# Logits folded into the scores and sums products of a routed decoder layer

## What is computed

```
x = x + linear_attention(layernorm(x))            # 8 heads of 64, elu + 1 features
x = x + cross_attention(layernorm(x), ctx) @ Wout + bout
h = layernorm(x)
logits = h @ Wg.T                                 # 8 experts
top_v, top_i = top_k(logits, 2); gates = softmax(top_v)
pos = cumsum(onehot(top_i)) - 1; keep = pos < 1280
x = x + sum over the two experts of gate * expert(h)   # gelu(h W1a) * (h W1b) @ W2
```

## Time and profile before

| | us |
|---|---|
| runs: median (lowest to highest of 3) | 1612.87 (1607.64 to 1614.09) |
| the profiled execution | 1614.39 |
| its span, first to last instruction | 1612.7 |

### The profile page before, as it was taken

The page is one execution under the profiler, slowest core; times in us unless marked ns, Lnnn a source line. Parts: engine busy times, 40 slices in busy tenths (PEclk is TensorE's granted clock), DMA queues, the critical chain, the costliest instruction groups (busy, mean ns, idle before and its releaser), DMA issues.

```text
span 1612.7 us, 21589 instructions
## 1 busy us (share of the span) xinstructions
PE 1507.6 (93%) x7686; PEld 1271.4 (79%) x7687; DVE 662.7 (41%) x1393; ACT 542.6 (34%) x881; POOL 360.3 (22%) x354
## 2 busy tenths in 40 slices
PE   6999999899998549999999989999999999999998
PEld 5778877788876338788888968888978978898886
DVE  6635555576777614331143243114532332214311
ACT  5334333244433414331143243124432332124311
POOL 3213123135543520201211220121121121021011
PEclk9999999998998569999999999999999999999999
DMA  9101222044424431521233252123452162024122
GB/s 190 53 1 52 80 79 105 1 157 132 99 85 131 131 105 54 157 60 31 37 121 91 52 145 70 33 33 117 124 159 46 36 175 46 20 52 130 22 43 26
DMA packets 78987, 132.23 MB, mean 82 GB/s; under 512 B 30388, under 2 KB 30516, under 8 KB 77912
## 3 DMA queue, kind: packets, MB, share of 16 engines
q1 hardware_dynamic: 62520, 97.40, 20.6%
q0 software_dynamic: 16416, 34.16, 11.4%
HBM read 93.63 MB, written 37.91 MB: 82 GB/s over the span
## 4 chain that ended last, share of the span: by engine, by line
PE 82%; DVE 5%; issue 3%; DMA 3%; POOL 3%; ACT 2%; another core or an unknown queue 1%; SPq 0%; ACTq 0%; POOLq 0%; DVEq 0%
PE pg L877 15%; PE pg L878 15%; PE pg L879 15%; PE pj L877 9%; PE pj L879 8%; PE pj L878 8%; PE pj L1079 2%; POOL slot_table L574 2%; PE pg L1048 1%; PE pg L1128 1%; PE pt L1226 1%; DMA stage<-w 1%; DVE w_lo L1289 1%; PE pt L1070 1%
## 5 line engine op out<-in xcount | busy, mean ns | idle before, releaser
L877 PE MATMUL pg<-xe_hi,w_hi 128*128 128x512 f32 (+2 forms) x1088 | 393.9, 362 | 22.4 <-issue 10.6
L878 PE MATMUL pg<-xe_lo,w_hi 128*128 128x512 f32 (+2 forms) x1088 | 393.1, 361 | 0.0
L879 PE MATMUL pg<-xe_hi,w_lo 128*128 128x512 f32 (+2 forms) x1088 | 392.6, 361 | 0.0
L1641 DVE TENSOR_TENSOR hp<-gl,pg 128x512 f32<-128x512 f32 (+1 forms) x136 | 87.1, 641 | 606.1 <-ACT gl L830 596.1
L632 POOL DMA_INDIRECT out_rows<-ost,etab x62 | 100.3, 1618 | 800.0 <-ACT ost L857 396.3
L877 PEld LDWEIGHTS pg<-xe_hi,w_hi 128*128 128x128 f32 x1088 | 207.6, 191 | 54.2 <-issue 12.2
L879 PEld LDWEIGHTS pg<-xe_hi,w_lo 128*128 128x128 f32 x1088 | 207.7, 191 | 28.3
L830 ACT ACTIVATE gl<-pg 128x512 f32<-128x512 f32 (+1 forms) x136 | 76.1, 560 | 457.0 <-PE pg L879 452.7
L878 PEld LDWEIGHTS pg<-xe_lo,w_hi 128*128 128x128 f32 x1088 | 207.5, 191 | 28.3
L877 PE MATMUL pj<-w_hi,hg_hi 128*128 128x512 f32 x464 | 183.4, 395 | 0.0
L879 PE MATMUL pj<-w_hi,hg_lo 128*128 128x512 f32 x464 | 180.8, 390 | 0.0
(11 more groups left out here) (220 smaller groups left out, 2067.6 us busy)
## 6 DMA issues: line engine op xcount, KB each, us to landing
stage<-w SPq DMA_DIRECT2D x96, 512.0 KB, 5.2
xr<-x SPq DMA_DIRECT2D x8, 1024.0 KB, 7.6
out_rows<-xr SPq DMA_DIRECT2D x8, 1024.0 KB, 4.7
x_rows<-xn SPq DMA_DIRECT2D x8, 1024.0 KB
x_in<-x SPq DMA_DIRECT2D x7, 1024.0 KB, 5.2
late_xT<-xT_hi SPq DMA_DIRECT2D x2, 1024.0 KB, 3.9
late_xT<-xT_lo SPq DMA_DIRECT2D x2, 1024.0 KB, 6.0
xT_hi<-late_xT SPq DMA_DIRECT2D x2, 1024.0 KB, 6.1
```

Of the source, the lines that this page charges most:

```text
L877: nc.tensor.matmul(o, lh, rh, start=start, stop=False)
L878: nc.tensor.matmul(o, lh, rl, start=False, stop=False)
L879: return nc.tensor.matmul(o, ll, rh, start=False, stop=stop)
L1641: v.tensor_tensor(hp[j % 2][:, 0:w], gl[j % 2][:, 0:w], pg[:, 2 + j % 2, 0:w], ALU.mult).then_inc(s_hp, 1)
```

## The change

The logits are linear in x2, and x2 is x1 plus the cross attention's output, so they are now taken in two parts. `wgp` stands in eight spare columns of `wqk` beside the 77 score columns (the product was 96 wide before and still is), so `scores` gives the part of x1. `slg` holds, beside the mask factor `emask`, the products of `vp` with `wgp`, so the sums product (nine columns instead of one) gives the part of the cross attention, still to be divided by the sum. VectorE puts both together (`logits`). x2 is no longer turned; `xT3`, `turn_and_route` and `logits_out` go. `turn_vp` and `value_logits` make `slg` once, in the front.

With the logits there before x2 is, routing, positions, slots and pack of group g all stand in turn g of the loop instead of g+1, the scatter in turn g+1 instead of g+2. The order is new on TensorE, VectorE, ScalarE and POOL, the late jobs' places too.

```diff
-LATE_AT = {(-1, 0): [0], (0, 0): [1], (0, 1): [2], (0, 2): [3], (1, 0): [4], (1, 1): [5], (1, 2): [6],
-           (2, 0): [7], (2, 1): [8], (2, 2): [9], (3, 0): [10], (3, 1): [11], (3, 2): [12],
-           (4, 0): [13], (4, 1): [14], (5, 0): [15]}
+LATE_AT = {(-1, 0): [0], (-1, 2): [1], (0, 0): [2], (0, 1): [3], (0, 2): [4], (1, 0): [5], (1, 1): [6],
+           (1, 2): [7], (2, 0): [8], (2, 1): [9], (2, 2): [10], (3, 0): [11], (3, 1): [12], (3, 2): [13],
+           (4, 0): [14], (4, 1): [15]}
...
                 for q in range(2):
-                    if g == 2 * q:
+                    if g == q:
 
                         sp.wait_ge(s_proj, JA + (q + 1) * KC)
...
             for g in range(GROUPS):
-                if g >= 2:
-                    scatter(g - 2)
+                if g >= 1:
+                    scatter(g - 1, range(0, TI * TOPK - 2))
+                late_q(late(g - 1, 2))
+                if g + 1 < GROUPS:
+                    if g >= 1:
+                        scatter(g - 1, range(TI * TOPK - 2, TI * TOPK))
+                    rstd_1(g + 1)
                 late_q(late(g, 0))
-                late_q(late(g, 1))
-                if g + 1 < GROUPS:
-                    rstd_1(g + 1)
-                else:
-                    scatter(g - 1)
                 norm3(g)
                 if g + 1 < GROUPS:
                     sigma(g + 1)
-                late_q(late(g, 2))
-            scatter(GROUPS - 1)
+                else:
+                    scatter(g - 1, range(TI * TOPK - 2, TI * TOPK))
+                late_q(late(g, 1))
+            scatter(GROUPS - 1, range(TI * TOPK))
...
             for g in range(GROUPS):
+                turned(sT[:], 0)
+                late_q(late(g - 1, 2))
                 if g >= 1:
                     normalise3(g - 1)
...
                 if g + 1 < GROUPS:
-                    turned_rows(xT2, range(TI), 1)
-                    late_q(late(g, 2))
...
+                    turned_rows(xT2, range(2), 1)
+                    late_q(late(g, 0))
+                    late_q(late(g, 1))
+                    turned_rows(xT2, range(2, TI), 1)
+                    if g == GROUPS - 2:
+                        for s in range(4):
+                            split(0, s)
+                    gate_exp(g)
                     score_exp(g + 1)
+            gate_exp(GROUPS - 1)
             normalise3(GROUPS - 1)
...
+            def sums(g, at):
 
                 b = g // NG
                 pe.wait_ge(s_btev, at)
-                if g:
-                    pe.wait_ge(s_posev, g)
                 for i in range(TI):
-                    ins = mm(pj[0][:, i:i + 1], sT[:, i * P:(i + 1) * P], emask[:, b:b + 1], start=True, stop=True)
+                    ins = mm(pj[0][:, i * (1 + EX):(i + 1) * (1 + EX)], sT[:, i * P:(i + 1) * P], slg[:, b, :],
+                             start=True, stop=True)
                 ins.then_inc(s_sum, 1)
...
-            late_q(late(-1, 0), -1)
             attend(0, range(2))
             keys_values(1)
             attend(0, range(2, TI))
+            late_q(late(-1, 0))
             pe.wait_ge(s_kvev, 2)
-            at_x1 = turn_x1(0, range(2), 0)
-            scores(0, at_x1, range(2))
-            at_x1.update(turn_x1(0, range(2, TI), 0))
-            scores(0, at_x1, range(2, TI))
+            at_x1 = turn_x1(0, range(TI))
+            scores(0, at_x1)
+            attend(1, range(2))
+            late_q(late(-1, 2))
             for g in range(GROUPS):
                 more_groups = g + 1 < GROUPS
-                if more_groups:
-                    attend(g + 1, range(2))
                 at_e = turn_exp(g)
-                late_q(late(g, 0), g)
-                if g:
-                    positions(g - 1)
                 if more_groups:
                     attend(g + 1, range(2, TI))
-                late_q(late(g, 1), g)
+                sums(g, at_e)
+                late_q(late(g, 0))
                 if more_groups:
-                    at_x1 = turn_x1(g + 1, range(2), 1)
-                values(g, at_e)
+                    at_x1 = turn_x1(g + 1, range(2))
+                    late_q(late(g, 1))
+                    positions(g)
+                values(g, range(2))
                 if more_groups:
-                    scores(g + 1, at_x1, range(2))
-                    at_x1.update(turn_x1(g + 1, range(2, TI), 1))
-                    late_q(late(g, 2), g)
-                    scores(g + 1, at_x1, range(2, TI))
-                turn_and_route(g)
-            positions(GROUPS - 1)
+                    at_x1.update(turn_x1(g + 1, range(2, TI)))
+                values(g, range(2, TI))
+                if more_groups:
+                    scores(g + 1, at_x1)
+                    if g + 2 < GROUPS:
+                        attend(g + 2, range(2))
+                    late_q(late(g, 2))
+                else:
+                    positions(g)
...
+            def logits(g):
+
+                dve.wait_ge(s_sum, g + 1)
+                both = pj[0][:, 0:TI * (1 + EX)].rearrange("p (i c) -> p i c", c=1 + EX)
+                v.reciprocal(sinv[:], both[:, :, 0])
+                v.tensor_copy(lgs[:], both[:, :, 1:1 + EX]).then_inc(s_sinv, 1)
+                dve.wait_ge(s_sinv, g + 1)
+                link(v.tensor_tensor(lgs[:], lgs[:], sinv[:].unsqueeze(2).broadcast_to([P, TI, EX]), ALU.mult))
+                v.tensor_tensor(lg[:], lgs[:], lgx[g % 2][:], ALU.add).then_inc(s_lg, 1)
...
             for g in range(GROUPS):
-                if g >= 1:
-                    logits_out(g - 1)
-                    route(g - 1)
...
+                more_groups = g + 1 < GROUPS
+                if more_groups:
                     attention_out(g + 1, 0)
...
+                logits(g)
+                route(g)
+                if more_groups:
+                    attention_out(g + 1, 1)
+                    positions_out(g)
                 cross_out(g)
...
+                if more_groups:
                     score_stats(g + 1)
+                else:
+                    positions_out(g)
+                slots(g)
+                gate_diff(g)
+                if more_groups:
                     softmax(g + 1)
...
+                gates(g)
+                pack_tokens(g)
```

More of the change, by code:

```diff
@@ L569, in norm3, with scatter @@
                 p.tensor_tensor(shift[1][:], neg_mean[1][:], rstd[1][:], ALU.mult).then_inc(s_rstd3, 1)
-            def scatter(g):
+            def scatter(g, columns):
                 pool.wait_ge(s_dest, g + 1)
-                for c in range(TI * TOPK):
+                for c in columns:
                     p.indirect_dma_start(
@@ L934, in xattn_values, with turn_vp, value_logits @@
                 ins.then_inc(s_xset, 1)
+            def turn_vp():
+                pe.wait_ge(s_vpev, 1)
+                for b in range(NB):
+                    for m in range(KC):
+                        ins = nc.tensor.transpose(pt[b][:, m * CK:(m + 1) * CK],
+                                                  vp[:, b * D + m * P:b * D + (m + 1) * P], ident[0:CK, 0:CK])
+                ins.then_inc(s_xset, 1)
+            def value_logits():
+                pe.wait_ge(s_xev, 3)
+                for b in range(NB):
+                    for m in range(KC):
+                        ins = mm(pt[0][0:CK, b * EX:(b + 1) * EX], vpT[:, b, m * CK:(m + 1) * CK], wgp[:, m, :],
+                                 start=m == 0, stop=m == KC - 1)
+                ins.then_inc(s_xset, 1)
             def project(s):
@@ L952, in project @@
                         xattn_values()
+                    if s == 2 and j == TI:
+                        turn_vp()
+                    if s == 2 and j == TI + 1:
+                        value_logits()
                     if s or j >= 2:
@@ L1061, in bank, with turn_x1 @@
                 return pt[k]
-            def turn_rows_of(src, done, g, tiles, first):
+            def turn_x1(g, tiles):
                 at = {}
                 for i in tiles:
-                    if done is not None:
-                        pe.wait_ge(done, g * TI + i + 1)
-                    to = bank((first + i) % 2)
+                    pe.wait_ge(s_x1, g * TI + i + 1)
+                    to = bank((1 + i) % 2)
                     for k in range(KC):
-                        ins = nc.tensor.transpose(to[:, k * P:(k + 1) * P], src[:, i, k * P:(k + 1) * P], ident[:])
+                        ins = nc.tensor.transpose(to[:, k * P:(k + 1) * P], xr[g % 4][:, i, k * P:(k + 1) * P],
+                                                  ident[:])
                     ins.then_inc(s_bt, 1)
```

154 lines of the change are left out of this document (60 added, 94 removed).

## The result

The changed kernel is slower: 1626.8 us (median of 5 runs, 1622.2 to 1630.4) against 1612.9, ratio 1.0092 with a 95% interval of 1.0064 to 1.0119. I had forecast 1574, range 1557 to 1600. The profiled execution took 1626.2 us; its span is 1624.5 us, against 1612.7 before.

A forecast was written before the change was run, and what follows sets the result against it. TensorE was taken to bound the first five periods, mutual waits the last two. 311.9 + 5 x 26.3 + 2 x 27 + 47 = 544.4 us to the expert stage, 38.5 less, giving 1574 us, range 1557 to 1600.

The forecast's parts named there:

- that stage itself unchanged at 1029.8 us: Expert stage, after the attention stage: the change would leave its length at 1029.8 us.
- the stage or the front giving back the gain: Rival: expert stage or front gives back the gain; within 0.5% of before only if 30 us went there; chance 0.02.
- the case that I gave 0.25: Rival in the scores stage: engines wait for one another again, all seven periods 29.7 us, 1596 in all; chance 0.25.
- my own sign: Scores stage: `nbias` intervals over 29 us, dips within late jobs, or a `dest` wait in every group would show it wrong.
- the walk: Step-by-step timing of one scores-stage period across engines: 26.3 us with late jobs, against 30.7 on average before.
- the stall of the second late job: In each late-job period TensorE waits 1.9 us for ScalarE to read the first late job's bank.
- goes with the products: TensorE's clock dip, some 2 to 3 us a group, would vanish with the `wgp` products, leaving 1.00 in late-job periods.
- The Trainium skill's reading: Rival: x1's remaining turns keep the dips in five late-job periods, 2.6 us each, 13 more, 1587; dips case chance 0.2.
- The removed work: TensorE, scores stage: turning x2 and its `wgp` product take 5.8 us in every group, with nothing under it.
- Both near 23: Work per period: TensorE 22.4 us with three late jobs, VectorE 23.3, so how they wait for each other counts.
- TensorE has no gap there, so +2.6: Front: 8 turns of `vp` and 16 small products add 2.6 us to TensorE's path; first `nbias` at 311.9 us.
- Periods without late jobs and tail: Last two periods 27 us each, between 23.5 and 31.6 at half clock; last `nbias` to expert stage 47 us, 12 less.

The follow-up runs named there:

- Four kernels: Idle instructions added ahead of ScalarE's expert loop: changed kernel with 32 more 1601.0 us, 16 more 1600.7; kernel before with 96 more 1644.3, 64 more 1613.7.
- after +32: The changed kernel with 32 idle instructions added on ScalarE just ahead of its expert loop: 1601.0 us, ratio 0.9919 to the kernel before.
- after: The changed kernel as first measured, against the kernel before: 1626.8 us, ratio 1.0092.
- the kernel with ScalarE's new order: Changed kernel with 32 idle ScalarE instructions, plus ScalarE reading the first late job's bank before copying out x1's two turned tiles: 1592.3 us, timed once.
- the dummy work: Turns of x1 and narrow products, results unread, added on TensorE to the kernel with all four edits: 1601.4 us, ratio 0.9906.
- the two runs with idle instructions: The kernel before with 96 or 64 idle instructions added on ScalarE ahead of its expert loop: 1644.3 and 1613.7 us.
- The later kernels with this edit: Values' logits products moved one query job later in the front; added to the kernel with ScalarE's new order: 1580.2 us once, 1585.2 in rounds.
- all four edits: Changed kernel with 32 idle ScalarE instructions, ScalarE's swapped order, GpSimd's new order and later values' logits: 1582.4 us, ratio 0.9789 to the kernel before.
- the kernel with filled waits: All four edits, plus unread products of wq filling TensorE's wait for the exponentials in periods 0 to 5: 1587.9 us, ratio 0.9822.

## Why the prediction was wrong

**The expert stage, 28.4 of the 50.3 us.** The step that failed is "that stage itself unchanged at 1029.8 us": I read it off the diff, which changes nothing in it, and gave 0.02 to the stage or the front giving back the gain, "say by splits or table loads late". It was neither, but the place of ScalarE's loop code, moved by the 32 copies that the change removes ahead of it: 1058.2 us measured. Four kernels show it. Nothing else of the change slows the stage: with 16 or 32 idle instructions it is 1028 to 1029 us. Why one place is slow and another isn't stays open.

**The sign.** Without that one term the changed kernel is at 0.9919, 1600 us by the ratio, at the upper end of my range and near the 1596 of the case that I gave 0.25, that the queues give the gain back. It is not that case, though: it had all seven periods at 29.7, and in after +32 they take 27.2 to 31.0 and, the last two, 26.2 and 27.2. The other terms took the gain from 38.5 us to 13.

**The five late-job periods, 14.1 us.** By my own sign the walk is wrong here, with three of the five over 29 us. What it named was there: the stall of the second late job was 1.89 us in period 0 (1.9 walked). It missed three things.
- VectorE's small operations took their clean durations in the sum, while in their new places GpSimd's additions fall on them: 1.1 us a period, shown twice. The kernel before has one such case at `sig`, 1.23 us at 433.11, and I had not read it.
- The clock. I had taken it that the dip "goes with the products", and 1.00 in all five. The products went, and three of the five periods still fell (0.89, 0.94, 0.94), now behind TensorE's waits, of which it has more. That the old dips came with the turns and narrow products is not refuted by this: put back as a dummy, they have falls right behind them with TensorE busy throughout. One cause was exchanged for another. The price is smaller than the 2.6 us that I gave it: a period at 0.94 takes 29.3 us in after against 28.8 at 1.00, and 28.0 against 28.0 in the kernel with ScalarE's new order; at 0.88 or 0.89 it takes 1.6 to 2.2 us more (29.6 and 31.0). The Trainium skill's reading ("TensorE: Matmul & The Clock Gate", Part 4) gave the right forecast, that the falls would stay. The trace fits it, with 0.50 at 342:344 behind the dummy work, but no run here parts the turns from the narrow products.
- The stall again. With the held operations gone a period at full clock takes 26.9 us, where the walk less its stall gives 24.4. The walk laid the stall to ScalarE's order and would lose it all by the swap; in that period it is still 2.16 us. Less it 24.7 are left, within 0.3 of the walk. Here ScalarE gets the first late job's bank late by the rows (the last section has the rows of one case), and why stays open.

**The removed work.** Its worth was set too high: 38 us of it cost 10.5 when put back, because VectorE, 22 to 25 us busy a period, stands right behind TensorE. "Both near 23" in the walk said so, and should have widened the range below the gain of 38.

**The front, 6.5 us.** "TensorE has no gap there, so +2.6" summed durations and missed whom the new products wait for: VectorE's copy is queued behind 2.9 us of normalising, hence 2.68 us of waiting and a job at half clock. 3.9 us, shown. Of the other 2.6 some 1.6 are there ahead of the new work (the last key product ends at 118.9 us in after, at 117.3 in before), and the start is not that steady: the kernel before has its first `nbias` at 308.7 and 310.7 in the two runs with idle instructions. The later kernels with this edit have it at 312.4 to 314.3, 0.5 to 2.4 above the forecast.

**Periods without late jobs and tail** were right: 54.2 for 54, 48.1 for 47, with half clock where the forecast had it (0.75 and 0.64). The 27 was a choice between 23.5 and 31.6, so its closeness is partly luck; the tail's parts came out too, the wait at the last `dest` with 3.1 us for 2.8.

## What to carry to other kernels

An engine's code ahead of a loop that is run many times is part of the loop's cost: where a change removes or adds instructions there, look at the idle time by "issue" at the loop's head and at the packets of the instruction queues, and try a few idle instructions before judging the change. The same holds for an experiment that adds instructions: here it made 7 to 9 us of one result and most likely 4.5 of another. In the change itself it turned a gain of 0.8% into a loss of 0.9%. Once the bound engine has been relieved down to the next one, the order of the others is what is left: two swapped lines on ScalarE and three on GpSimd, and one block a job later in the front, brought the changed kernel to 0.979 of the kernel before (1582.4 us; 1580.7, ratio 0.9786, with the 224 idle instructions on TensorE, which is the same within the intervals).

## What the runs showed of the hardware

- ScalarE: a loop of 286 instructions (my count) costs 28 us in eight rounds, by its place alone: 40 fetches of 8192 bytes instead of 4 or 5, in after 8.2 to 9.1 us of standing at seven heads of eight. TensorE: 19 fetches of 16384 bytes instead of 9, 7 to 9 us.
- TensorE's clock fell in two situations: behind a wait (2.42 us at 347.40 in after, 1.33 at 395.68 with all four edits), though not behind every one (none behind 2.96 us at 418.18 in after), and right behind 16 turns and 32 rows of 8-column products with no wait at all (0.50 at 342:344 in the kernel with the dummy work).
- A VectorE operation of 0.16 us with two operands in SBUF takes 1.25 us beside a GpSimd addition of 1.28.
- Open: some of TensorE's products end later than their rows say. In the kernel with all edits the turns behind a late job begin, by their row, at 345.33, but ScalarE gets that job only at 347.19:

```profile
345.33 1.04 PE L1089 MATMUL pt<-ident,xr 128*128 128x128 f32 x8
```

```profile
347.19 0.69 ACT L744 ACTIVATE fe<-pj,bq_neg 128x512 f32<-128x512 f32 x1 [2.53 <-remote]
```

In the kernel with filled waits the same wait was 3.8 us. I have not found its cause. It is most of what the periods at full clock take beyond the walk: 2.16 us of stall in one where the walk without ScalarE's old order has none.
